# Taking the pause out of TensorE's list of score pieces, and copying the turned row of maxima on ScalarE

## What is computed

```
x = x + tanh(g_xattn[0]) * L0_xattn(layernorm(x), ctx, ctx, energy)     # long, plain
x = x + tanh(g_ffn[0])   * L0_ffn(layernorm(x))
x = x + tanh(g_xattn[1]) * L1_xattn(layernorm(x), ctx)                  # a local one (256 keys) and a long one
x = x + tanh(g_ffn[1])   * L1_ffn(layernorm(x))
x = x + tanh(g_xattn[2]) * L2_xattn(layernorm(x), ctx)                  # long, plain
x = x + tanh(g_ffn[2])   * L2_ffn(layernorm(x))
x = x + tanh(g_xattn[3]) * L3_xattn(layernorm(x), ctx, ctx, mask)       # long, masked
x = x + tanh(g_ffn[3])   * L3_ffn(layernorm(x))
# each attention, per head: softmax(q @ k.T * scale) @ v, 256 queries, 256 or 1601 keys
```

## Time and profile before

| | us |
|---|---|
| median of 3 runs | 1785.07 (1784.7 to 1787.7) |
| the profiled execution, its own time | 1786.3 |
| its span | 1783.6 |
| TensorE busy | 1568.4 (88%) |
| VectorE busy | 1344.5 (75%) |
| ScalarE busy | 1174.2 (66%) |
| GpSimd busy | 142.1 (8%) |

### The profile page before, as it was taken

How to read it: one execution, slowest core, us unless ns; L and a number is a source line. 1 busy time by engine, 2 the same in 40 slices (tenths; PEclk the granted TensorE clock), 3 DMA queues, 4 the chain that set the end, 5 groups by cost and what they waited for, 6 DMA issues and landing times.

```text
span 1783.6 us, 45505 instructions
## 1 busy us (share of the span) xinstructions
PE 1568.4 (88%) x15403; PEld 652.6 (37%) x15403; DVE 1344.5 (75%) x2285; ACT 1174.2 (66%) x2201; POOL 142.1 (8%) x231
## 2 busy tenths in 40 slices
PE   5789999978778999996997799999778999999867
PEld 3422222246232222224675122222453333333345
DVE  4689999745769999974784899999347777777358
ACT  3368888842545888883894488888443666666636
POOL 4000000012000000002121000000100000000012
PEclk9889999989897999997899699999887999999979
DMA  8922222205542222220115322222172211111001
GB/s 275 292 77 76 91 76 75 83 1 150 182 134 61 91 76 75 90 60 12 48 61 154 118 76 76 91 75 62 38 230 62 62 60 60 60 61 60 29 13 36
DMA packets 91729, 156.46 MB, mean 88 GB/s; under 512 B 15623, under 2 KB 41758, under 8 KB 91646
## 3 DMA queue, kind: packets, MB, share of 16 engines
q1 hardware_dynamic: 86846, 145.54, 26.4%
q0 software_dynamic: 1792, 4.66, 0.8%
q10 hardware_dynamic: 3008, 5.13, 0.8%
HBM read 119.13 MB, written 35.14 MB: 86 GB/s over the span
## 4 chain that ended last, share of the span: by engine, by line
PE 55%; DVE 18%; issue 11%; DMA 6%; SPq 5%; ACT 2%; POOL 1%; DVEq 0%; ACTq 0%; POOLq 0%
PE pv_bank L1512 17%; DVE mx L1063 12%; PE exp_ring L1478 10%; PE score_ring L1464 9%; DMA qp<-ms 4%; PE exp_ring L1493 4%; PE score_ring L1664 3%; PE exp_ring L1675 3%; PE exp_ring L1496 2%; DMA k_d<-k2c 2%; SPq L529 2%; PE score_ring L1403 1%; PE score_ring L1577 1%; PE exp_ring L1410 1%; ACT early L835 1%
## 5 line engine op out<-in xcount | busy, mean ns | idle before, releaser
L835 ACT ACTIVATE early<-exp_ring 128x512 f32<-128x512 f32 (+1 forms) x1728 | 930.6, 597 | 328.4 <-PE exp_ring L1478 172.7
L1063 DVE TENSOR_REDUCE mx<-score_ring 128x2 f32<-128x802 f32 (+2 forms) x832 | 764.5, 966 | 71.2 <-PE score_ring L1464 56.3
L1464 PE MATMUL score_ring<-kp,qp 64*128 64x401 f16 (+4 forms) x2688 | 503.1, 350 | 71.8 <-DVE mx L1063 47.6
L1512 PE MATMUL pv_bank<-early,vg 128*32 128x256 f32 (+1 forms) x6912 | 557.6, 393 | 2.9 <-issue 2.0
L1478 PE MATMUL exp_ring<-qp,kp 64*128 64x512 f16 (+2 forms) x1312 | 366.2, 390 | 17.9 <-DMA qp<-ms 16.2
L1464 PEld LDWEIGHTS score_ring<-kp,qp 64*128 64x128 f16 (+2 forms) x2688 | 155.8, 100 | 270.3 <-DVE mx L1063 160.0
L1512 PEld LDWEIGHTS pv_bank<-early,vg 128*32 128x32 f32 (+1 forms) x6912 | 140.5, 108 | 209.9 <-issue 122.4
L1478 PEld LDWEIGHTS exp_ring<-qp,kp 64*128 64x128 f16 (+2 forms) x1312 | 92.0, 95 | 308.0 <-ACT early L835 241.9
L661 POOL COPY vg<-v_all 128x416 f32 (+1 forms) x48 | 25.4, 533 | 884.4 <-PE pv_bank L1512 833.4
L1493 PE MATMUL exp_ring<-qp,kp 64*64 64x512 f16 x832 | 86.4, 403 | 6.9 <-issue 3.7
L1056 DVE CUSTOM_DVE_ANT_0 wfcT<-score_ring,mask_add 128x802 f16<-128x802 f32 x64 | 63.6, 994 | 32.2 <-PE score_ring L1464 25.6
(11 more groups left out here) (241 smaller groups left out, 1243.9 us busy)
## 6 DMA issues: line engine op xcount, KB each, us to landing
kp<-k_d SPq DMA_DIRECT2D x128, 400.2 KB, 3.2
qp<-q_d SPq DMA_DIRECT2D x160, 256.0 KB, 3.3
k_d<-k1c SPq DMA_DIRECT2D x32, 400.2 KB, 8.2
ctxT<-ctxT_d SPq DMA_DIRECT2D x12, 800.5 KB, 6.0
k_d<-k2c SPq DMA_DIRECT2D x16, 400.2 KB, 9.2
q_d<-qp ACTq DMA_DIRECT2D x1, 4096.0 KB, 23.0
ctxT_d<-ctxT SPq DMA_DIRECT2D x4, 800.5 KB, 9.3
o_all<-in_ctx SPq DMA_DIRECT2D x4, 768.0 KB
```

Source lines behind the costliest of these rows:

```text
L835: act.activation(pt[g][0:rows_, 2 * h:2 * h + 2, :], bank[0:rows_, :].rearrange("p (i q) -> p i q", q=S), ACT.Exp).then_inc(exped, 1)
L1063: dve.tensor_reduce(dst, src, AX.X, ALU.max).then_inc(score_free, 1)
L1464: ins = pe.matmul(pa[slot][q, z, 0:w], qp1[par][rows_, i, qt * P + q.start:qt * P + q.stop], kp1[par][rows_, at:at + w], start=True, stop= ...
L1512: ins = pe.matmul(po[R * j:R * j + R, 0:S], vg[par][0:rows_, s, j, :], pt[g][0:rows_, j, :], start=(s == 0), stop=(s == r.kt - 1))
```

## The change

In the four long runs the two empty places of `todo` go: 17 places are spread over the 26 fills. The copy of the turned row goes from VectorE's list into ScalarE's: behind the exponentials of the eleventh key tile (`s == r.kt - 3`) ScalarE waits for the turn (`m_turned`), copies the row and counts `ms_ok`. For a run's first unit it does so ahead of the first exponential. SyncE waits for `ms_ok`. A long unit counts 16 instead of 17 in `score` and `score_free`, since the turn and its copy have semaphores of their own. Who takes the turn's bank next (the piece two places behind the turn, and the heads' output at a run's end) waits for `ms_ok` too. The last turn of a run takes the bank of place 3 instead of bank 1. The local run stays as it is.

```diff
-PAUSE = 2
...
-        self.pause = 0 if self.local else PAUSE
...
+        self.rows0 = before.rows0 + UNITS * (not before.local) if before else 0
+        self.use0 = before.use0 + UNITS * (before.uses if before.local else before.c) if before else 0
...
+    def done(self, n, k, first=False):
+
+        if self.local:
+            return self.use0 + (k - (k > self.turn) if first else n * self.uses - 1 + k) + 1
+        return self.use0 + (0 if first else n * self.c) + k - (k > self.turn) + 1
+
+    def free(self, n, k, first=False):
+
+        if self.local or first:
+            return FREE_SCORE + self.done(n, k, first) - 2
+        return FREE_SCORE + self.use0 + n * self.c + k - 1 - (k - 2 >= self.turn)
...
SyncE, loads, unit:
-                    sp.wait_ge(score_free, FREE_SCORE + (r.use(n + 1, r.turn) if p2 else
-                                                         r.use0 + UNITS * r.uses - 1) + 1)
+                    if r.local:
+                        sp.wait_ge(score_free, FREE_SCORE + (r.done(n + 1, r.turn) if p2 else
+                                                             r.use0 + UNITS * r.uses))
+                    else:
+                        sp.wait_ge(ms_ok, r.rows0 + n + 1)
                     maxima(n, par)
...
ScalarE, attention:
+                def keep_rows(par, slot, n):
+
+                    act.wait_ge(m_turned, r.rows0 + n + 1)
+                    act.activation(ms[par][:, :], pa[slot][:, 0, :].bitcast(F16)[0:HG, 0:S], ACT.Copy
+                                   ).then_inc(ms_ok, 1)
+
+                def unit(n, par, prev=True, last=False):
                     for s in range(r.kt):
...
                         if s == r.lag - 1 and prev:
                             evac(n - 1)
+                        if s == r.kt - 3 and not r.local and not last:
+                            keep_rows(1 - par, r.slot(par, r.turn), n + 1)
+
+                if not r.local:
+                    keep_rows(0, r.slot(1, r.turn), 0)
                 unit(0, 0, prev=False)
...
VectorE, attention, unit:
                         if j is None:
-                            keep_rows(1 - par, r.slot(par, k), r.use(n, k))
+                            if r.local:
+                                keep_rows(1 - par, r.slot(par, k), r.done(n, k))
...
TensorE, attention:
-                    ins.then_inc(score, 1)
+                    ins.then_inc(score if r.local else m_turned, 1)
...
                     if k == r.turn:
                         pe.wait_ge(m_ok, r.u0 + n)
-                        turn(1 - par, slot, use)
+                        turn(1 - par, slot, r.free(n, k))
                         return
                     j = k - (k > r.turn)
-                    pe.wait_ge(score_free, use + FREE_SCORE - 1)
+                    pe.wait_ge(score_free, r.free(n, k, first))
+                    if k - 2 == r.turn and not first and not r.local:
+                        pe.wait_ge(ms_ok, r.rows0 + n)
...
-                        todo += [None] * r.pause + [(2, k) for k in range(r.ahead)]
+                        todo += [(2, k) for k in range(r.ahead)]
...
                                     pe.wait_ge(m_ok, r.u0 + UNITS)
-                                    turn(1, 1, r.use0 + UNITS * r.uses - 1)
+                                    if r.local:
+                                        turn(1, 1, FREE_SCORE + r.use0 + UNITS * r.uses - 2)
+                                    else:
+                                        turn(1, r.slot(0, r.turn), FREE_SCORE + r.use0 + UNITS * r.c)
```

More of the change, by code:

```diff
@@ L96, in __init__ @@
         self.shift0 = before.shift0 + UNITS // 2 * before.shifts if before else 0
-        self.use0 = before.use0 + UNITS * before.uses if before else 0
+        self.rows0 = before.rows0 + UNITS * (not before.local) if before else 0
+        self.use0 = before.use0 + UNITS * (before.uses if before.local else before.c) if before else 0
         self.fill0 = before.fill0 + UNITS * before.fills if before else 0
@@ L131, in back @@
         return next(d for d in range(1, 9) if self.banks[f - d] == self.banks[f])
-    def use(self, n, k, first=False):
-        return self.use0 + (k - (k > self.turn) if first else n * self.uses - 1 + k)
+    def done(self, n, k, first=False):
[6 more added lines that the diff above has]
+        return FREE_SCORE + self.use0 + n * self.c + k - 1 - (k - 2 >= self.turn)
     def slot(self, par, k, first=False):
@@ L355, in flamingo @@
         score, score_free = sem("score"), sem("score_free")
-        mx_done, m_ok = sem("mx_done"), sem("m_ok")
+        mx_done, m_ok, m_turned, ms_ok = sem("mx_done"), sem("m_ok"), sem("m_turned"), sem("ms_ok")
         mask_t, mask_e, prep_m, mask_x = [sem(n) for n in ("mask_t", "mask_e", "prep_m", "mask_x")]
@@ L824, in evac @@
                     act.activation(o_all[:, n, :], po[:, 0:S], ACT.Copy).then_inc(o_ok, 1)
-                def unit(n, par, prev=True):
+                def keep_rows(par, slot, n):
[3 more added lines that the diff above has]
+                def unit(n, par, prev=True, last=False):
                     for s in range(r.kt):
@@ L844, in attention @@
                     unit(2 * t + 2, 0)
-                unit(UNITS - 1, 1)
+                unit(UNITS - 1, 1, last=True)
                 evac(UNITS - 1)
@@ L1050, in piece @@
                     src = pa[r.slot(par, k, first)][:, :, 0:w]
-                    dve.wait_ge(score, r.use(n, k, first) + 1)
+                    dve.wait_ge(score, r.done(n, k, first))
                     if r.mask:
-                        dve.wait_ge(score_free, r.use(n, k, first) + (k != r.turn + 1))
+                        dve.wait_ge(score_free, FREE_SCORE + r.done(n, k, first) - 2)
                         dve.sem_inc(passed, 1)
@@ L1065, in keep_maxima @@
                 def keep_maxima(n, par, first):
-                    dve.wait_ge(score_free, FREE_SCORE + r.use(n, r.uses - 1, first) + 1)
+                    dve.wait_ge(score_free, FREE_SCORE + r.done(n, r.uses - 1, first))
                     if r.mask:
@@ L1075, in keep_maxima, with keep_rows @@
                                           ALU.max, negate=True).then_inc(m_ok, 1)
-                def keep_rows(par, slot, use):
-                    dve.wait_ge(score, use + 1)
+                def keep_rows(par, slot, ready):
+                    dve.wait_ge(score, ready)
                     dve.tensor_copy(ms[par][:, :], pa[slot][:, 0, :].bitcast(F16)[0:HG, 0:S]
@@ L1095, in attention @@
                 unit(UNITS - 1, 1)
-                keep_rows(1, 1, r.use0 + UNITS * r.uses - 1)
+                if r.local:
+                    keep_rows(1, 1, r.use0 + UNITS * r.uses)
             def heads_out(r):
@@ L1435, in attention, with turn @@
             def attention(r):
-                def turn(par, slot, use):
-                    pe.wait_ge(score_free, use + FREE_SCORE - 1)
+                def turn(par, slot, free):
+                    pe.wait_ge(score_free, free)
                     for qt in range(QT):
@@ L1441, in turn @@
                                            m16[par][:, qt, :], ident16[:, :])
-                    ins.then_inc(score, 1)
+                    ins.then_inc(score if r.local else m_turned, 1)
                 def piece(n, par, k, first=False, half=0):
-                    use, slot = r.use(n, k, first), r.slot(par, k, first)
+                    slot = r.slot(par, k, first)
                     if k == r.turn:
                         pe.wait_ge(m_ok, r.u0 + n)
-                        turn(1 - par, slot, use)
+                        turn(1 - par, slot, r.free(n, k))
                         return
                     j = k - (k > r.turn)
-                    pe.wait_ge(score_free, use + FREE_SCORE - 1)
+                    pe.wait_ge(score_free, r.free(n, k, first))
+                    if k - 2 == r.turn and not first and not r.local:
+                        pe.wait_ge(ms_ok, r.rows0 + n)
                     if j == 0:
@@ L1569, in heads_out @@
                 if tiles[0] == 0:
-                    pe.wait_ge(score_free, FREE_SCORE + r.use0 + UNITS * r.uses)
+                    pe.wait_ge(score_free, FREE_SCORE + r.use0 + UNITS * (r.uses if r.local else r.c))
+                    if not r.local:
+                        pe.wait_ge(ms_ok, r.rows0 + UNITS)
                 pe.wait_ge(o_ok, FREE_PV + r.u0 + (tiles[-1] // QT + 1) * HG)
```

## The result

| | median us | ratio to the kernel before (95% interval) |
|---|---|---|
| kernel before | 1784.91 | |
| changed kernel | 1803.81 (1801.15 to 1806.03) | 1.0101 (1.0088 to 1.0113) |
| forecast | 1782.9 (1774 to 1793) | |

The change makes the kernel 18.9 us slower, where I forecast 1782.9, 2.2 less than the 1785.07 on which that was made, and gave "slower" a chance of 0.25. The profiled execution took 1801.15, its span 1799.3 against 1783.6: 15.7 more.

A forecast was written before the change was run, and what follows sets the result against it. The chain through the turned row's copy and DMAs closes unmasked units; TensorE bounds the masked run. Unmasked units +1.3, masked run -6.0, run ends +3.1, run starts -0.6: -2.2 us, from 1785.07 to 1782.9; range 1774 to 1793.

The forecast's parts named there:

- the journey: From the end of the turned row's copy, through SyncE's DMAs, to the next unit's first fill: 2.49 us.
- (b): Unmasked units: ScalarE's copy ends at 14.17 us, next first fill at 16.66 to 16.68; +0.03 a unit, +1.3 us.
- (c): Masked run, bound by TensorE: tile 11 -0.37, tile 10 -0.12, tile 7 +0.06; -0.43 us a unit, -6.0 us.
- the join: VectorE's step behind a unit's maxima, ahead of piece 0's maximum; forecast to start 10.28 us behind the first fill.
- it doesn't do what it says: Rival: in the masked run piece 0's bank makes tile 9 lose what tile 11 gains; 1789 us, chance 0.12.
- (d): Ends of runs: copy 0.90 us later, about 0.4 in the masked run, +3.1 us; starts 0.15 earlier, -0.6 us.
- (e): New waits: ScalarE on `m_turned` costs nothing; TensorE's piece 5 on `ms_ok` has 0.2 us of cover.
- Slower: ScalarE's copy is long or late: Rival: ScalarE's copy takes 0.5 to 0.6 us or sits behind a late exponential; about 1794 us, chance 0.18.

The follow-up runs named there:

- e3: Changed kernel with VectorE's list of the long runs written out instead of a loop over pairs; 1790.75 us, 1.0041 of the kernel before.
- e6: Changed kernel, but VectorE copies the row, its list is written out, and the 17 places are set by hand; 1747.35 us, 0.9811 of the kernel before.
- e9: Kernel before with VectorE's list of the long runs written out instead of a loop; 1783.07 against 1782.06 us, 1.0008.

## Why the prediction was wrong

The mechanism that I named was right: the period is closed by the row, not by either busy engine. The waits for `qp<-ms` rose, if to 29.8 and not over 30, the copy took 0.36, within 0.03 of my 0.39, the journey stayed at 2.49, and the last units came 0.9 later (16.01 against 15.12). The sum failed on terms of (b) and (c).

*(b), tile 2: missing.* I took tile 2, now with one piece, at the 1.06 of a single tile. It takes 1.40, since its product waits for the eviction, a wait that I put at nothing. That moves every later piece and the join: 10.62 instead of the 10.28 of my working, +0.34 a unit. I had weighed the new waits that the change writes down, and not those that it lays bare.

*(b), join to piece 0: mis-sized.* I took 0.22 from the start of a run; it is 0.12 or 0.53, in turn, and e3 shows why. The row that I read stands outside the loop. In rows 4 the same place has 0.55 of idle time, which I put down to the pause alone. Mean +0.1 a unit.

*(b), the rest of the chain: right.* From the start of piece 0's maximum to tile 10's first fill I had 1.89 (10.50 to 12.39), measured 1.90 (617.39 to 619.29); from there to the copy's end 1.78, measured 1.75 (to 621.04). With these the hand working gives 16.67 + 0.34 + 0.10 + 0.01 - 0.03 = 17.09, and 17.08 is measured, so nothing in the unmasked unit is left open. Against before (16.65) that is 0.43 a unit, 42 x 0.43 = 18 us. In the profiled executions of the two kernels the three runs differ by 16.6: 16.1 in the second to fourteenth units, 2.6 in the last ones, -2.1 in the first ones.

*(c), the masked run: the gain is there in every second unit and eaten in the others.* Forecast -0.43 a unit, -6.0 us; measured 20.89 and 21.58 in turn, 21.27 in the mean of units two to thirteen, against 21.23 before, and 0.2 us more for the run. The short units have nearly the whole of it: tile 10 takes 1.40 and tile 11 1.47, as worked out. In the long ones tile 9 takes 2.38 instead of the 1.9 of a double tile, and tile 11 stays at 1.89. TensorE's timeline has a wait in each:

```profile
1492.88 0.53 PE L1488 MATMUL score_ring<-kp,qp 64*64 64x401 f16 x4 [0.37 <-DVE mx L1076]
...
1497.20 0.41 PE L1517 MATMUL exp_ring<-qp,kp 64*64 64x512 f16 x4 [0.35 <-ACT early L851]
```

The first is piece 2 behind the loop's end and is gone in e3 (21.02 a unit, half of the gain back). The second is a fill of tile 12 that needs an exponential of tile 11; by the code the ring of three banks is bent at the end of a pair of units. It stays in e3, and no run separates it. So the failed step of (c) is tile 11 at a plain 1.46 in every unit, and tile 9 without a new wait. My rival "it doesn't do what it says" had the outcome and the place (tile 9 loses what tile 11 gains), for 0.12.

Together: 0.40 a unit more than the +0.03 forecast, 42 x 0.40 = 17 us, and the masked run's 6 are about the 21 us between 1782.9 and 1803.81.

*(d) and (e)* held: ends +0.9 each (masked +0.25 for 0.4), the copy at a run's start 0.16 nearer to the turn (masked 0.6), no wait at `m_turned` in a unit, none at `ms_ok`.

*The rivals.* "Slower: ScalarE's copy is long or late" had the right place and the wrong reason: I looked for the price in the copy's length, where it was as forecast, and said that it decides from +0.14 a unit. It was +0.43, and from work ahead of the turn. The range ended at 1793, so it missed by 11 us. It was built as if the hand working were exact to 0.1 a unit; but with 42 like units, one overlooked wait of 0.3 is 13 us. The Trainium skill's rule that simple arithmetic (it names `relu`, `max`, `min`, `add` and `mul`) goes on VectorE ("ScalarE: Activation LUTs", Rules for kernel authors) agrees with the runs without the pause, where VectorE's copy is ahead by 1.6%, and with the pause nothing can be told (1.0007). Its budget of about 0.3 us and 0.83 ns an element is for an ACTIVATE whose bias is a pointer operand, which this copy, by its line of code, doesn't have, so my estimate of 0.51 was not for this instruction; the trace has 0.357. ScalarE lost because exponentials stand ahead of the copy in its list.

## What to carry to other kernels

An empty place in one engine's list can be cover for something on another, here a loop's end. And taking it out spreads the places that stay, so that a tile can lose the second piece that covered an eviction. Before taking it out, look at what runs in it on every engine, in two periods that follow one another, as a loop over pairs shows in every second one only. If a period is closed by a small step with a long journey behind it, put that step on the engine that is free at that moment and has nothing ahead of it in its list; its total load says little, as long as that step is what closes the period: in e6 it no longer is. And with tens of like periods, a range should allow for one wait that was not seen.

## What the runs showed of the hardware

The end of VectorE's loop costs 0.41 us between two instructions that have their data (0.53 against 0.12 from start to start of the join and the next maximum), and nothing in the kernel before, where VectorE is idle there anyway (e9). ScalarE's copy of 4 partitions x 256 numbers took 0.357 and VectorE's 0.27. The two DMAs of the row took 2.47 to 2.52 us from the copy's end to the fill in the second long run in every order that was tried and in which the fill waited for them. In these runs it was a fixed price; whether it can be shortened, no run tried.
